# Causal attention on one core: value projections taken out of the opening and given to the turns in quarters, query heads alternated between the two row halves

## The reference

```python
def attention(x, wq, wk, wv, wo, bo):
    b, t, _ = x.shape                      # 2, 1024
    q = (x @ wq).reshape(b, t, HEADS, HEAD_DIM)      # 16 heads of 16
    k = (x @ wk).reshape(b, t, HEADS, HEAD_DIM)
    v = (x @ wv).reshape(b, t, HEADS, HEAD_DIM)
    scores = jnp.einsum('bqhd,bkhd->bhqk', q, k)
    mask = jnp.arange(t)[:, None] < jnp.arange(t)[None, :]
    scores = jnp.where(mask, -jnp.inf, scores)
    attn = jax.nn.softmax(scores / np.sqrt(HEAD_DIM), axis=-1)
    ctx = jnp.einsum('bhqk,bkhd->bqhd', attn, v).reshape(b, t, EMB)
    return ctx @ wo + bo
```

## Time and profile before

| | us |
|---|---|
| median of 3 runs (lowest, highest) | 2356.11 (2355.21, 2358.67) |
| the profiled execution's own time | 2360.74 |
| its span | 2359.0 |
| PE / DVE / ACT / POOL busy in the span | 1966.9 / 1593.2 / 904.7 / 455.7 |

### The profile page before, as it was taken

One profiled execution on the slowest core, in us unless ns is written; L12 is line 12 of the kernel. 1 busy time (PEld: TensorE's weight loads), 2 busy tenths in 40 slices (PEclk: granted clock), 3 DMA queues, 4 the chain that ended last, 5 costly groups with the idle time before them and its releaser, 6 DMA issues. The chain is left out here.

```text
span 2359.0 us, 28355 instructions
## 1 busy us (share of the span) xinstructions
PE 1966.9 (83%) x9864; PEld 1246.2 (53%) x9864; DVE 1593.2 (68%) x3414; ACT 904.7 (38%) x1689; POOL 455.7 (19%) x320
## 2 busy tenths in 40 slices
PE   7999999699999988856766386546899999999997
PEld 4543443488888856433433243323354444369997
DVE  4676773544445344779999999997368786356775
ACT  2365665222222222431112111101437665546765
POOL 1011111623133030001001100110001111115765
PEclk9788888899999999878887698777879996889999
DMA  6032321311110010200000000000203232128885
GB/s 178 13 65 46 77 48 33 125 36 54 36 53 18 0 54 9 79 1 10 10 1 8 18 9 9 0 0 4 60 15 66 54 77 42 33 87 247 233 222 119
DMA packets 60158, 132.73 MB, mean 56 GB/s; under 512 B 18952, under 2 KB 29960, under 8 KB 57216
## 3 DMA queue, kind: packets, MB, share of 16 engines
q1 hardware_dynamic: 50688, 118.17, 18.5%
q0 software_dynamic: 8832, 12.16, 3.0%
q10 hardware_dynamic: 512, 0.79, 0.2%
HBM read 91.27 MB, written 10.98 MB: 43 GB/s over the span
## 5 line engine op out<-in xcount | busy, mean ns | idle before, releaser
L779 DVE CUSTOM_DVE_ANT_0 pair<-pair,a_mask 128x512 f32<-128x512 f32 (+3 forms) x768 | 408.4, 587 | 174.9 <-PE pair L596 172.4
L751 ACT ACTIVATE a_prob<-pair 128x512 f32<-128x512 f32 (+3 forms) x768 | 329.3, 490 | 208.1 <-PE pair L622 203.7
L622 PE MATMUL pair<-a_qx,a_kx 50*128 50x512 f32 (+3 forms) x768 | 273.8, 457 | 8.6 <-ACT a_prob L751 7.5
L596 PE MATMUL pair<-a_kx,a_qx 48*128 48x512 f32 (+3 forms) x768 | 268.5, 437 | 14.6 <-DVE a_mx_raw L779 8.5
L622 PEld LDWEIGHTS pair<-a_qx,a_kx 50*128 50x128 f32 x768 | 131.6, 210 | 220.4 <-ACT a_prob L751 125.1
L636 PE MATMUL pair<-a_prob,a_v 128*17 128x512 f32 (+3 forms) x1536 | 189.7, 569 | 34.0 <-ACT a_o_all L756 28.6
L544 POOL TENSOR_SCALAR_AFFINE_SELECT a_prob<-a_prob 128x512 f32<-128x512 f32 x128 | 89.4, 699 | 649.1 <-ACT a_prob L751 648.8
L1016 DVE TENSOR_TENSOR m_h<-pair,m_g 128x512 f32<-128x512 f32 x96 | 66.4, 691 | 210.7 <-PE pair L839 209.5
L1398 PE MATMUL pair<-h_stream,r_w_kz 128*128 128x512 f32 x192 | 103.9, 695 | 118.7 <-DVE r_region L1804 113.4
L837 PE MATMUL pair<-m_x_hi,m_w_lo 128*128 128x512 f32 x448 | 178.4, 398 | 26.3 <-POOL m_w_lo L901 24.1
L838 PE MATMUL pair<-m_x_hi,m_w_hi 128*128 128x512 f32 x448 | 177.2, 395 | 0.0
(11 more groups left out here) (314 smaller groups left out, 4110.2 us busy)
## 6 DMA issues: line engine op xcount, KB each, us to landing
mx_raw<-in_L_ffn_experts SPq DMA_DIRECT2D x69, 512.0 KB, 4.7
m_raw<-in_L_cond_experts SPq DMA_DIRECT2D x18, 1024.0 KB, 4.9
a_qx<-a_comp SPq DMA_DIRECT2D x104, 96.0 KB, 2.8
a_kx<-a_comp SPq DMA_DIRECT2D x48, 192.0 KB, 4.4
a_factor<-a_inverses SPq DMA_DIRECT2D x56, 128.0 KB, 2.7
r_w_ring<-in_r_q_w SPq DMA_DIRECT2D x8, 512.0 KB, 3.9
m_raw<-in_L_cond_experts SPq DMA_DIRECT2D x6, 512.0 KB, 3.6
token_rows<-mx_h_rows SPq DMA_DIRECT2D x2, 1040.0 KB, 7.7
```

The costliest lines, as they stand in the source:

```text
L596: nc.tensor.matmul(first_bank[t % FR][:, 0:c1 - c0], qx[r, m % 2, a // 2, i * P:(i + 1) * P], kx[r, m % 3, a // 2, c0:c1], start=True, sto ...
L622: nc.tensor.matmul(score_bank[t % SR][:, q0:TT], kx[r, n % 3, a // 2, j * P:(j + 1) * P], qx[r, n % 2, a // 2, h * TT + q0:(h + 1) * TT], ...
L751: nc.scalar.activation(prob[:, i % RING, a, q0:TT], score_bank[t % SR][:, q0:TT], ACT.Exp, scale=SCALE).then_inc(s["b_exp"], 1)
L779: nc.vector.tensor_tensor_reduce(out=first_bank[t % FR][:, 0:cols], in0=first_bank[t % FR][:, 0:cols], in1=mask[:, m0:m0 + cols], scale=1. ...
```

## The change

1. **Value projections.** Only pair 0 (groups 0 and 1) is projected in the opening, now in four quarters of 256 tokens, all ahead of the first of the firsts. Pairs 1 to 3 are projected in quarters within turns 0 to 5, two a turn, behind steps 3 and 8, through the shared bank. `v_sb` becomes a ring of four groups, and the first values product of a turn waits for the last quarter's copy.
2. **Width of the values product.** VW goes from 17 to 32: the stationary operand has 32 columns a head (16 values, a one, 15 zeros).
3. **Row halves.** `FIRST` lists the heads innermost, so the firsts go 0, 1, 2, 3 over the heads instead of four or eight of one head, and `FIRSTS_AFTER` is another table.
4. **Places.** `VALUES_AFTER` is another table; the copy of the half's result stands on ACT behind the score product that follows the last values product of the half (behind (4, 1), was (5, 0)). In `SMALL` the second half of "qk" goes from step 5 to step 7, the first maxima from 6 to 5. `NORM` starts its steps two to four steps earlier.
5. **Twin.** The copy of L714 goes from ACT to POOL, which now also fills `kx` with ones for groups 1 and 2 behind twins.

```diff
-VW = HD + 1
+VW = SLOT
+QUARTERS = 4
 PRODUCT = 3 * HD
 ROWS = PRODUCT + 2
 
-FIRST = [(a, i, c_) for part in (range(4), range(4, QT)) for a in range(GH) for i in part for c_ in range(i // 4 + 1)]
+FIRST = [(a, i, c_) for part in (range(4), range(4, QT)) for i in part for c_ in range(i // 4 + 1) for a in (0, 1, 2, 3)]
...
-FIRSTS_AFTER = ((2, 0, 1, 1), (2, 2, 0, 1), (1, 0, 2, 0), (0, 3, 0, 0),
-                (1, 0, 2, 1), (2, 2, 1, 1), (2, 0, 3, 0), (1, 2, 0, 2),
-                (2, 0, 1, 1), (0, 3, 0, 0), (1, 2, 0, 2), (0, 0, 1, 0))
-
-
-VALUES_AFTER = (0, 3, 3, 3, 2, 0, 1, 2, 3, 3, 2, 3)
-
-
-SMALL = (("max", 0, 1), None, None, None, ("qk", 2, 0), ("qk", 2, 1), ("max", 1, 0), None, None, None, None, None)
+FIRSTS_AFTER = ((1, 2, 0, 0), (2, 2, 0, 2), (0, 1, 1, 1), (2, 0, 1, 1),
+                (1, 2, 1, 0), (1, 0, 3, 0), (3, 0, 0, 2), (1, 0, 0, 2),
+                (1, 1, 0, 2), (3, 0, 0, 1), (0, 2, 1, 0), (1, 3, 1, 0))
+
+
+VALUES_AFTER = (3, 3, 3, 1, 0, 1, 2, 1, 2, 3, 2, 1)
+
+
+SMALL = (("max", 0, 1), None, None, ("v", 0, 0), ("qk", 2, 0), ("max", 1, 0), None, ("qk", 2, 1), ("v", 0, 1), None, None, None)
...
-NORM = {3: 0, 5: 1, 8: 2, 9: 3, 10: 4}
+NORM = {1: 0, 2: 1, 4: 2, 6: 3, 8: 4}
...
-    values = [(pair, v) for pair in range(NG // 2) for v in range(2)]
+    for v in range(QUARTERS):
+        order += [("v0", v), ("v0_use", v)]
...
-        if f % 5 == 2 and values:
-            order += [("v", *values[0]), ("v_use", *values[0])]
-            values = values[1:]
...
+    copies = []
     for i in range(NS):
         for a in range(GH):
             order.append(("scores", n, i, a))
+            order += copies
+            copies = []
...
                 order.append(("values", n, i - 1))
+                copies = [("copy", n, 0)] if i == 4 else []
             elif a == VALUES_AFTER[i] and n:
-                order += [("values", n - 1, NS - 1), ("copy", n - 1, 1)]
-            if (i, a) == (5, 0):
-                order.append(("copy", n, 0))
+                order.append(("values", n - 1, NS - 1))
+                copies = [("copy", n - 1, 1)]
...
+            elif what == "v":
+                entry = (what, n // 2 + 1, 2 * (n % 2) + y)
...
-SHARED = ("qk", "max", "sums", "spread", "out")
+SHARED = ("qk", "v", "max", "sums", "spread", "out")
...
-        v_sb = c.sb(f"{tag}_v", [P, NG, QT, GH * VW], ctx=ctx)
+        v_sb = c.sb(f"{tag}_v", [P, 4, QT, GH * VW], ctx=ctx)
...
+                def ones(x):
                     nc.gpsimd.memset(kx[:, x, :, :].bitcast(F32), 1.0).then_inc(s["ones"], 1)
...
+                def twin(m, h):
+                    pool.wait_ge(s["hi"], m * HALF + h + 1)
+                    to = parts(m)[:, :, half(h)].bitcast(F32)
+                    nc.gpsimd.tensor_copy(to[:, 0, :], to[:, 2, :]).then_inc(s["twin"], 1)
+                    if m * HALF + h in (1, 2):
+                        ones(m * HALF + h)
...
+                nc.gpsimd.memset(v_sb[:, :, :, :].rearrange("p x t (a s) -> p (x t a) s", s=VW)[:, :, HD:HD + 1], 1.0)\
+                    .then_inc(s["v_ones"], 1)
+                nc.gpsimd.memset(v_sb[:, :, :, :].rearrange("p x t (a s) -> p (x t a) s", s=VW)[:, :, HD + 1:VW], 0.0)\
+                    .then_inc(s["v_ones"], 1)
+                does = {"qk": twin, "scores": select}
...
+                def values_of(bank, pair, v):
+                    m = 2 * pair
+                    for t in range(QT // QUARTERS):
+                        for k in range(KD):
+                            last = nc.tensor.matmul(bank[:, t * P:(t + 1) * P], c.h[:, k, time(m, (QT // QUARTERS * v + t) * P, P)],
+                                                    w[:, m % GROUPS, 1, k, :], start=k == 0, stop=k == KD - 1)
+                    return last
...
+                    values_of(take("v", pair, v), pair, v).then_inc(s["vp"], 1)
...
+                    if i == 0 and n > 1:
+                        pe.wait_ge(s["used"], used("v", n // 2, QUARTERS - 1))
...
-                    act.wait_ge(s["hi"], m * HALF + h + 1)
-                    nc.scalar.activation(to[:, 0, :], to[:, 2, :].bitcast(F32), ACT.Copy).then_inc(s["twin"], 1)
...
+                def copy_quarter(bank, pair, v):
+                    n = QT // QUARTERS
                     for x in range(2):
                         last = nc.scalar.activation(
-                            v_sb[:, 2 * pair + x, 4 * v:4 * v + 4, :].rearrange("p t (a s) -> p t a s", s=VW)[:, :, :, 0:HD],
-                            v_bank(pair, v).rearrange("p (t x a s) -> p t x a s", t=4, x=2, s=HD)[:, :, x, :, :], ACT.Copy)
...
+                    act.wait_ge(s["vp"], (pair - 1) * QUARTERS + v + 1)
+                    copy_quarter(bank_of("v", pair, v), pair, v).then_inc(s["used"], 1)
```

More of the change, by code:

```diff
@@ L326, in turn @@
                 entry = (what, x, y)
+            elif what == "v":
+                entry = (what, n // 2 + 1, 2 * (n % 2) + y)
             else:
                 entry = (what, n + x, y)
-            if entry[1] < NG:
+            if entry[1] < (NG // 2 if what == "v" else NG):
                 order.append(entry)
                 uses = [] if what == "begin" else finished(*entry)
-    order += uses
+    order += uses + copies
     assert closing or found == NF
@@ new lines, in select @@
+                def select(n, i, a):
+                    h, j = STEPS[i]
+                    if a < GH - 1 or j < 4 * h:
+                        return
+                    pool.wait_ge(s["b_exp"], (n * NS + i + 1) * GH)
+                    q0 = cut(h, j)
+                    block_ = prob[:, i % RING, :, q0:q0 + P]
+                    nc.gpsimd.affine_select(out=block_, in_=block_, compare_op=ALU.is_ge, fill=0.0, base=0,
+                                            pattern=[[0, GH], [1, P]], channel_multiplier=-1)\
+                        .then_inc(s["b_cut"], 1)
@@ new lines, in _ @@
+                ones(0)
+                nc.gpsimd.memset(v_sb[:, :, :, :].rearrange("p x t (a s) -> p (x t a) s", s=VW)[:, :, HD:HD + 1], 1.0)\
[3 more added lines that the diff above has]
+                does = {"qk": twin, "scores": select}
+                for what, *which in ORDER:
+                    if what in does:
+                        does[what](*which)
@@ L565, in qk_projection, with v_first @@
                     last.then_inc(s["proj"], 1)
-                def v_projection(pair, v):
-                    m = 2 * pair
-                    task = 2 * pair + v
-                    pe.wait_ge(s["used"], used("qk", 1, 1))
-                    if task >= len(v_banks):
-                        pe.wait_ge(s["v_used"], task - len(v_banks) + 1)
-                    bank = v_bank(pair, v)
-                    for t in range(4):
-                        for k in range(KD):
-                            last = nc.tensor.matmul(bank[:, t * P:(t + 1) * P], c.h[:, k, time(m, (4 * v + t) * P, P)],
-                                                    w[:, m % GROUPS, 1, k, :], start=k == 0, stop=k == KD - 1)
-                    last.then_inc(s["vp"], 1)
+                def values_of(bank, pair, v):
[5 more added lines that the diff above has]
+                    return last
+                def v_first(v):
+                    pe.wait_ge(s["used"], used("qk", 1, 1))
+                    values_of(v_banks[v], 0, v).then_inc(s["v0_mm"], 1)
+                def v_projection(pair, v):
+                    values_of(take("v", pair, v), pair, v).then_inc(s["vp"], 1)
                 def first(m, t):
@@ L635, in values @@
                         r = slice(a * SLOT, a * SLOT + VW)
[L636 removed]
+                        last = nc.tensor.matmul(value_bank[r, q0:TT], v_sb[:, n % 4, j, a * VW:(a + 1) * VW], prob[:, i % RING, a, q0:TT],
                                                 start=j == 0, stop=j == 4 * h + 3)
@@ L691, in out_projection @@
                     last.then_inc(s["om"], 1)
-                does = {"qk": qk_projection, "v": v_projection, "first": first, "max": maxima, "scores": scores,
+                does = {"qk": qk_projection, "v0": v_first, "v": v_projection, "first": first, "max": maxima, "scores": scores,
                         "values": values, "sums": sums, "spread": spread, "out": out_projection, "begin": begin_out}
```

39 lines of the change are left out of this document (14 added, 25 removed).

## The result

The changed kernel takes 2389.88 us (median of 4 runs, 2375.92 to 2406.92) against 2355.66 for the kernel before (4 runs): ratio 1.0161, 95% interval 1.0109 to 1.0212. It is 1.6% slower; forecast were 2251 us and a range of 2225 to 2310. The profiled execution of the changed kernel took 2402.61 us, 41.9 more than that of before, so the profile shows a difference somewhat larger than that of the medians (34.2). Ratios and their intervals leave out executions over 1.5% above the fastest of the same kernel (five of the ten of b_copy_rows), medians do not, so a ratio can differ a little from the quotient of the medians given with it.

The account below looks back on a forecast made before the run. PE was taken to bound the turns, with a stall for a copy bringing half clock. Gains of 50 (turns 1 to 5), 18 (turn 6), 19 (turn 0), 5 (turn 7) and 13 (openings) made 105 us: 2251 us, range 2225 to 2310.

Parts of the forecast that it names:

- What bounds the kernel, and the stall: Middle turns: PE sets their length; its 2.07 us wait for a copy at a half's end also brings half clock.
- The opening: First of the firsts to first score product: 37.0 to 30.5 us, gain 6.5 in each attention, 13 in all.
- A turn at full clock: A middle turn of the changed kernel: from 35.2 to 34.4 us, summed from separate terms.
- The stall's 2.1: At a half's end in a turn: PE no longer waits for the half's copy, -2.1 us.
- The quarters: Two quarters of value projections come into each turn: 16 products of 128 columns, +2.2 us.
- The twin: Copy moved from ACT to POOL: 0.45 to 0.7 us there, nothing but the next triangle waiting behind it.
- The 0.5 for the queries: Turn's start: later keys and queries leave slack of 0.6 us; +0.5 us a turn, bounds 0 and 2.
- The 0.5 for the triangle: In a turn: earlier (3, 1) and (4, 0) values products may catch the triangle late, +0.5 us.
- Row halves, -1.9: Score and first products in a turn: 12 fewer neighbours on the same half, -1.9 us, from 0 to 4.1.
- The sum, without and with the clock: Whole kernel: turns 1 to 5 gain 50 us, turn 6 18, turn 0 19, turn 7 5, openings 13: 105.
- PE is starved of clock: Paired products and DVE's pace in the opening keep PE at half: turns 61 us, time 2600; chance 0.04.
- The first rival: The clock falls elsewhere in the turns: average 0.90, 37.4 us a turn, time 2300; chance 0.20.

Follow-up runs that it names:

- b_copy_rows: The kernel before with both single edits, the half's copy earlier on ACT and the firsts with heads innermost: 2370.08 us, ratio 0.9987.
- b_copy: The kernel before with only the half's copy placed earlier on ACT, behind the last exponential of step 4: 2285.99 us, ratio 0.9740.
- a_fill_end: The changed kernel with the last eight firsts of each group but the first issued twice: 2394.53 us, ratio 1.0208.
- a_places: The changed kernel with every table of before; short opening, quarters behind steps 3 and 8, width 32, twin on POOL and earlier copy stay: 2348.35 us, ratio 1.0000.
- b_copy_twin: b_copy with the twin on POOL as in the change: 2304.02 us, ratio 0.9743.
- a_qk6: The changed kernel with the second half of "qk" behind step 6 instead of 7: 2404.63 us, ratio 1.0198.
- a_order: The changed kernel with `FIRST` as before, heads one by one, and all else kept: 2381.21 us, ratio 1.0181.
- b_rows: The kernel before with only the firsts reordered, heads innermost, all tables as before: 2411.12 us, ratio 1.0286.
- a_fill_half: The changed kernel with every second first of every group but the first issued twice: 2357.33 us, ratio 1.0079.
- a_places_17: a_places with the values product 17 wide again and four extra products in the opening filling the value bank: 2337.94 us, ratio 0.9915.
- a_places_light: a_places with the quarters of values behind steps 2 and 10 instead of 3 and 8: 2370.61 us, ratio 1.0054.
- a_places_fill: a_places with the last 12 firsts of each later group issued twice: 2381.02 us, ratio 1.0111.
- b_copy_rows_fill: b_copy_rows with every second first of every group but the first issued twice: 2387.16 us, ratio 1.0194.
- a_fill_more: a_fill_half with all firsts of group 0, in the opening, issued twice too: 2368.78 us, ratio 1.0079.

## Why the prediction was wrong, by its own steps

**What bounds the kernel, and the stall: right.** The prediction held the copy's stall for the cause of the half clock and some 60 us for the clock's part of the gain. b_copy removes the stall and no more: 61 us less (0.974), most middle turns 33.0 to 33.6 at 1.00. In the profiled executions turns 0 to 6 of both attentions are 74 us shorter; 20.6 of these are the stalls of the middle turns themselves, so some 50 are clock. A stall doesn't always bring the fall: turn 1 of the second attention has one and stays at 1.00.

**The opening: right.** From 47.7, where the firsts began before, to the first score product: 30.0 us against 30.5 forecast. From the first projection to the first score product it was 47.4 and 49.0 us in the two attentions and is 41.0 and 42.3: 13.1 won, 13 forecast. DVE is dense, its L806 busy 23.64 of 24.70 us:

```profile
53.00:77.70 24.70, 23.64 (x91) 0.59 0.33 61
```

**A turn at full clock: right in sum.** The forecast was 34.4. No middle turn of the changed kernel is at full clock throughout, so what it would be is an estimate: 44.4 us at 0.73 hold 24.0 at half; less 0.44 x 24 it is 33.8. a_fill_end's 35.9 with eight more products, at up to 0.34 each, bears it out. The stall's 2.1 are gone, and so is the last turn's 1.33. The quarters cost about 2.6 (a_places against b_copy; 2.2 forecast). The twin is hidden (0.61 on POOL, 0.45 to 0.7 forecast; b_copy_twin). The 0.5 for the queries was more than they cost: they were 0.71 late in one turn of each attention, and it cost nothing that a_qk6 could give back. The 0.5 for the triangle didn't come: no product of the middle turns waits for POOL. *Row halves, -1.9*: with the tables of before the new order gives nothing at full clock (31.4 against 31.2 in turn 6 of b_copy_rows and b_copy_twin); DVE's pace takes what the pairs save, as the 4.9 us of waits for it show. With the new tables the term was about right by this estimate: 33.8 is some 2 us less than the 36.2 of a_places and the 36.6 of a_order, which have the added work without the new order. The saving was there to be had while the clock is full; what the order does to the clock was left out.

**The step that failed: "The sum, without and with the clock", turns 1 to 5 and turn 6.** It put the half clock of these turns at nothing, 34.4 and 30 us, as if the stall were the only thing that could bring the clock down. The two forecasts of -50 and -18 came out as +49.5 and +16.7. The same step gave turn 0 -19 (it came to -7.7: some 25 us of it are at half, not 10).

What the runs show in its place: 24 of the 44.4 us of each middle turn are at half clock, and the edit that was booked as a gain, the row halves with their order of the firsts, is one that lowers the clock. Alone it costs 2.9% (b_rows); on the kernel without the stall it takes back 2.5% (b_copy_rows), though it adds no product. In the changed kernel 24 more products a turn bring the clock back and shorten most middle turns by 7 us (a_fill_half), so too much work for PE isn't what costs. The wait for the queries isn't either (a_qk6). The order of firsts alone isn't all (a_order 1.0181): the tables that came with it must go too (a_places 1.000, by which order and tables together are worth 1.6%). How much of this each table has was not taken apart, nor which of the order's properties does it.

That is not the whole distance. From the early copy alone (b_copy, 0.974) to the changed kernel (1.0161) it is 4.2%, and 2.6 of it are there already in a_places, with the tables of before. What a_places adds to b_copy is the short opening, the quarters, the width and the twin. The quarters' 2.6 us in 12 turns are 31 us, the openings give back some 13, and the whole is 61; the rest, some 43, is clock by this estimate, for a reason that stays open.

**The rivals.** Nearest is the second, *PE is starved of clock*, which had 0.04. Its price was too high: the clock isn't at half throughout, but 24 us of each middle turn, twice the 12 from which it decides; 34.4 + 0.44 x 24 = 45.0 against 44.4 measured. That the pairs are what starves PE, as it says, isn't shown apart from the widths and the waits that came with the order. The ground against it, that the clock had come back after some 13.8 us "with nothing done for it", was the mistake: that was true of the old order of products, and the change altered just that order. In the changed kernel it comes back in the middle turns only behind the projection of queries and keys, and turn 6, which has none, stays at 0.51 for 47.3 us. The first rival's question, why turn 6 of before stood at 0.59, was a hint that was passed over, if a mixed one: that turn has a wait of 0.7 us for the copy too, and in b_copy it is at 0.81.

**Still open.** Why a_places is at 0.80 to 0.84 in most middle turns and b_copy at 1.00. The width (a_places_17) may be a part, the quarters' place isn't (a_places_light), more work at the turn's end doesn't help (a_places_fill). Whether the alternation, the grouping by width or the waits for DVE make b_rows slow. And what in a series of products the clock answers to: of the extra products those of a_fill_half raised it to full, those of b_copy_rows_fill a little, those of a_fill_more in the opening and of a_places_fill not.

## What to carry to other kernels

Before a change that spreads PE's work thinner or runs products side by side is booked as a gain, look at the granted clock of stretches that are thin already: a turn that stands at 0.59 with PE busy 40.5 of 41.7 us is a warning for the edit too. Test the parts of a change one at a time; here two numbers (the place of one copy) were worth 2.6% and a reordering in the same change cost as much. A reordering that is named for one property can change others; here it also moved the narrow products together. And when a kernel seems slow by clock, the same kernel with more work can tell it from one that is slow by work: if it gets faster, work wasn't the limit. If it doesn't, nothing is shown (b_copy_rows_fill, a_places_fill).

## What the runs showed of the hardware that was not expected

- In the changed kernel the clock fell with PE idle 0.58 of 8 us, in pieces of 0.15 to 0.17 where the trace names a releaser, and then stood at half for some 24 us with PE busy nearly throughout. The Trainium skill, "TensorE: Matmul & The Clock Gate", section "A second HAM failure mode: psum-queue depth-cycling", tells of a clock that goes up and down where TensorE is idle shortly and often between its products; this trace agrees in that no long idle stood before the fall.
- 24 more products of up to 512 columns a turn made nine of ten middle turns 7 us shorter (44.4 to 37.3), clock 0.73 to 1.00.
- Executions of one and the same kernel differ by the clock that they are granted: of 19 of the kernel before, the shortest took 2340.95 us at a mean clock of 0.887 and the longest 2386.07 at 0.863; the ten of b_copy_rows go from 2336.38 at 0.877 to 2412.90 at 0.831.
- The opening with 48 firsts at DVE's pace runs at 0.59, and with every one of them twice (PE busy 26.25 of 27.00 us) at 0.54: more products of this kind did not raise it. (The first is the changed kernel's opening, the second that of a_fill_more.)
